# Exponentials straight out of PSUM for the last five tiles of a decoder block's expert stage

## The reference

```
q = (x @ Wq + bq) as 8 heads of 64;  q = batchnorm(q)
q0, q1 = l2norm(q[..., :32]), l2norm(q[..., 32:])
s0, s1 = q0 . k0, q1 . k1                      # 32 scores each, per token and head
ts0, ts1 = the 4 largest of s0, of s1
w  = softmax over the 16 sums ts0[i] + ts1[j]
out = sum over heads and (i, j) of w * gelu(down[i*32+j] . x) * up[i*32+j]
```

## Time and profile before

| what | us |
|---|---|
| three runs | 439.9, 440.02, 441.66; median 440.02 |
| the profiled execution, its own time | 441.61 |
| its span, first to last instruction | 439.6 |
| busy: TensorE, VectorE, ScalarE, GpSimd | 406.9, 307.1, 228.6, 206.7 |
| mean granted TensorE clock | 0.984 of full speed |

### The profile page before, as it was taken

One profiled execution on the slowest core, in us unless ns is written; L12 is line 12 of the kernel. 1 busy time (PEld: TensorE's weight loads), 2 busy tenths in 40 slices (PEclk: granted clock), 3 DMA queues, 4 the chain that ended last, 5 costly groups with the idle time before them and its releaser, 6 DMA issues. The chain is left out here.

```text
span 439.6 us, 7801 instructions
## 1 busy us (share of the span) xinstructions
PE 406.9 (93%) x2579; PEld 371.9 (85%) x2579; DVE 307.1 (70%) x1133; ACT 228.6 (52%) x459; POOL 206.7 (47%) x201
## 2 busy tenths in 40 slices
PE   3998999978999999999999999999898978999786
PEld 2877788857899999999999999987686968999685
DVE  5899877568475576557647555575736698899995
ACT  3774546325565555445656443344555769675300
POOL 2588988922624234323332210001100659799991
PEclk9999999999999999999999999999999897999989
DMA  7700122002512222222222000000000000001011
GB/s 242 251 1 26 51 73 78 2 0 75 146 51 78 53 75 77 70 57 77 73 76 75 4 0 2 1 1 4 21 1 1 0 2 3 25 25 37 26 34 50
DMA packets 19991, 21.36 MB, mean 49 GB/s; under 512 B 3180, under 2 KB 16624, under 8 KB 19952
## 3 DMA queue, kind: packets, MB, share of 16 engines
q1 hardware_dynamic: 18832, 19.96, 15.4%
q10 hardware_dynamic: 1120, 0.92, 0.7%
HBM read 18.78 MB, written 2.10 MB: 47 GB/s over the span
## 5 line engine op out<-in xcount | busy, mean ns | idle before, releaser
L960 PE MATMUL att_pA<-context_cNh,att_pTh 128*128 128x256 f32 (+1 forms) x208 | 62.6, 301 | 1.0 <-DVE att_pTl L858 1.0
L961 PE MATMUL att_pA<-context_cNl,att_pTh 128*128 128x256 f32 (+1 forms) x208 | 58.3, 280 | 0.0
L962 PE MATMUL att_pA<-context_cNh,att_pTl 128*128 128x256 f32 (+1 forms) x208 | 58.1, 279 | 0.0
L1148 POOL TENSOR_TENSOR ffn_prod<-ffn_first,ffn_near 128x1024 f32<-128x1024 f32 (+1 forms) x29 | 54.7, 1885 | 6.4 <-DVE ffn_clamped L1499 5.9
L858 DVE TENSOR_TENSOR att_pTl<-att_pR,att_pTh 128x512 fp32r<-128x512 f32 x64 | 37.4, 586 | 26.7 <-ACT att_pTh L775 26.5
L877 DVE TENSOR_REDUCE att_mx<-keep_pQ 128x1 f32<-128x402 f32 x64 | 35.6, 568 | 25.5 <-PE keep_pQ L77 25.3
L765 POOL TENSOR_TENSOR context_cTl<-keep_raw,context_cTh 128x512 fp32r<-128x512 f32 (+1 forms) x24 | 23.1, 980 | 47.8 <-ACT context_cTh L789 47.8
L765 POOL TENSOR_TENSOR context_cNl<-keep_raw,context_cNh 128x512 fp32r<-128x512 f32 (+1 forms) x21 | 25.1, 1211 | 41.9 <-ACT context_cNh L789 41.9
L1634 PE MATMUL ffn_pT<-keep_ident,ffn_prod 128*128 128x128 f32 x256 | 34.8, 295 | 7.6 <-POOL ffn_prod L1148 6.3
L1634 PEld LDWEIGHTS ffn_pT<-keep_ident,ffn_prod 128*128 128x128 f32 x256 | 32.0, 153 | 10.8 <-DVE ffn_hT L1521 4.7
L960 PEld LDWEIGHTS att_pA<-context_cNh,att_pTh 128*128 128x128 f32 (+1 forms) x208 | 39.1, 188 | 2.2 <-DVE att_pTl L858 1.5
(11 more groups left out here) (302 smaller groups left out, 1145.6 us busy)
## 6 DMA issues: line engine op xcount, KB each, us to landing
keep_raw<-in_ctxT SPq DMA_DIRECT2D x24, 256.0 KB, 2.7
keep_raw<-in_ctx SPq DMA_DIRECT2D x24, 256.0 KB, 2.7
out<-keep_x SPq DMA_DIRECT2D x16, 128.0 KB, 1.7
keep_x<-in_x SPq DMA_DIRECT2D x3, 512.0 KB, 10.5
gru_wout<-in_W_out SPq DMA_DIRECT2D x1, 512.0 KB, 8.9
keep_raw<-in_fWq SPq DMA_DIRECT2D x2, 256.0 KB
keep_raw<-in_ctxT SPq DMA_DIRECT2D x8, 32.5 KB, 4.0
keep_raw<-in_ctx SPq DMA_DIRECT2D x4, 65.0 KB
```

The lines of the kernel that those rows point to most:

```text
L960: pe.matmul(pA[:, 0:D], l[0], r[0], start=(kt == 0), stop=False)
L961: pe.matmul(pA[:, 0:D], l[0], r[1], start=False, stop=False)
L962: last = pe.matmul(pA[:, 0:D], l[1], r[0], start=False, stop=(kt == CT - 1))
L1148: return eng.tensor_tensor(prod[:, i % PB, a:b].rearrange("p h (i j) -> p h i j", j=KEYS), (factor if factor is not None else first[:, n % ...
```

## The change

From tile 11 on (`RAISED_APART`), ScalarE takes the scores out of PSUM itself. It runs 16 exponentials of 128x32, one per head and half, each with that half's column of `ninv` as its scale, second halves first; then the Copy as before. VectorE's `scaled` is left out for these five tiles, and TensorE, before it overwrites a bank, waits for `raised` instead of `s_ready`. The wait for `near_ready` stands ahead of the branch, so it now comes before that for `s_ready` in the other tiles too.

```diff
--- before.py
+++ after.py
@@ -1120,6 +1120,7 @@
         SHARE = {LASTS - 1: HEADS // 2, LASTS: HEADS - 5, LASTS + 1: HEADS - 5}
         LATE_GELU = 6
         ADDED = TILES - WEIGH
+        RAISED_APART = 11
 
         def wait_squares(eng, n, chunks):
 
@@ -1290,9 +1291,23 @@
 
                 def exponentials(i):
                     n, t = i // PER, i % PER
-                    act.wait_ge(s_ready, i + 1)
                     if n >= 2:
                         act.wait_ge(near_ready, i - 2 * PER + 1)
+                    if i >= RAISED_APART:
+                        act.wait_ge(score_mm, i + 1)
+                        act.wait_ge(ninv_ready, [n in b for b in BATCHES].index(True) + 1)
+                        for part, done in ((1, e_ready), (0, raised)):
+                            for h in range(HEADS):
+                                g = 2 * h + part
+                                last = act.activation(e[:, n % 2, t, h, part * KEYS:(part + 1) * KEYS],
+                                                      pS[:, i % 2, g * KEYS:(g + 1) * KEYS], ACT.Exp,
+                                                      scale=ninv[:, i, g:g + 1])
+                            last.then_inc(done, 1)
+                        act.wait_ge(raised, i + 1)
+                        act.activation(e[:, n % 2, t, :, 0:KEYS], e[:, n % 2, t, :, 0:KEYS], ACT.Copy, scale=LIFT)\
+                            .then_inc(e_ready, 1)
+                        return
+                    act.wait_ge(s_ready, i + 1)
                     act.activation(e[:, n % 2, t, :, 0:KEYS], s[:, i % 2, :, 0:KEYS], ACT.Exp).then_inc(raised, 1)
                     act.activation(e[:, n % 2, t, :, KEYS:PAIR], s[:, i % 2, :, KEYS:PAIR], ACT.Exp).then_inc(e_ready, 1)
                     act.wait_ge(raised, i + 1)
@@ -1535,7 +1550,7 @@
                                                 *(inverse_norm_steps(k) for k in norm_batch if i > 2))
                     if i == TILES - 1:
                         steps = itertools.islice(final := weight_steps(n, 0, 1), 2)
-                    if 3 <= i + 1 < TILES:
+                    if 3 <= i + 1 < RAISED_APART:
                         scaled(i + 1)
                     dve.wait_ge(e_ready, 2 * i + 1)
                     largest(i, 1, steps)
@@ -1612,7 +1627,9 @@
 
                 def scores(i):
                     wait_query(pe, i // PER, QC)
-                    if i >= 2:
+                    if i - 2 >= RAISED_APART:
+                        pe.wait_ge(raised, i - 1)
+                    elif i >= 2:
                         pe.wait_ge(s_ready, i - 1)
                     for c in range(QC):
                         q = q0[:, c, i * P:(i + 1) * P] if i < PER else query(c, i * P, (i + 1) * P)
```

## The result

| | before | changed |
|---|---|---|
| median of the runs | 440.84 us (439.9 to 443.28, 4 runs) | 446.89 us (446.18 to 450.63, 4 runs) |
| ratio to before, 95% interval | 1 | 1.0114 [1.0061, 1.0167] |
| the same, a second series (e1 below) | 440.03 us (17 runs) | 447.64 us (6 runs), 1.0146 [1.0088, 1.0204] |
| profiled execution: time, span, granted clock | 441.61, 439.6, 0.984 | 450.63, 448.8, 0.973 |

The change makes the kernel slower, by the two ratios 5.0 and 6.4 us (the medians lie 6.1 and 7.6 apart). The forecast was 442.7 us with a range of 441.0 to 445.0: the sign was right, the size was not, and the time lies outside the range.

What follows compares the result with a forecast made beforehand. GpSimd was taken to set the pace after 379.79, 4.9 us a tile, fed by a chain through ScalarE and TensorE. Terms 0 + 1.3 + 1.36 = +2.7 us gave 442.7 us, range 441.0 to 445.0.

Steps and rivals of the forecast that it cites:

- the last bullet of Part 2: Tile 8: late exponential and squares make TensorE 0.9 us late, hidden by a longer stall at tile 11; 0.
- Part 2: Wait order in all tiles from 4 on: table load now stands behind the scaled scores; +1.3 us, all from tile 4.
- Part 3: Tile 11: sixteen exponentials ahead of the square root delay VectorE's reciprocal, so GpSimd's near is late; +1.36 us.
- Rival B: Second low clock stretch at TensorE's tile 8 norm sums; 2.6 for 1.36, or with late rise +4.8, 444.8 us; chance 0.16.
- Tile 4, forecast 1.3: Exponential of tile 4 starts 1.30 us later, delaying TensorE's sum of tile 1 and GpSimd; middle of 0.49 and 2.19.
- the forecast's upper case: Tile 4: clock stays low through the sum of tile 1 and eight score matmuls; TensorE late by 2.19 us.
- Its sign of being wrong: Last square root, tile 11: VectorE's reciprocal starting without a wait would show the sixteen-exponential step wrong.
- Part 1: VectorE's five scalings leave, 3.0 us of its time, absorbed by its waits for GpSimd's near; 0.
- Tile 6 and the rest of the order: Tile 6: its table load follows the GELUs, when the scores are already scaled; 0.
- A: Tile 4: clock rises at the same moment as before, 0.49+1.36 = +1.9, 441.9 us; chance 0.20.
- C: Table load does not wait behind the moved wait, exponentials every 0.12 us; 0 and 0.4, 440.4 us; chance 0.05.
- D: VectorE and not GpSimd is the bound, so its 3.0 us come back; faster, 437.0 us; chance 0.03.

Runs made afterwards that it cites:

- e1: The changed kernel run again without further edits, beside three variants on the same chip; 1.0146 of the kernel before.
- a1: Kernel before with only the wait order changed, near_ready called ahead of s_ready in every tile from 4 on; 1.0143 of the kernel before.
- a4: Kernel before with the two waits exchanged in tile 8 alone; 1.0090 of the kernel before.
- e2: Changed kernel with the old order of the two waits put back at tile 8 alone; 1.0082 of the kernel before.
- e4: Changed kernel with normalising and squares of group 6 moved ahead of the exponentials of tile 8; 1.0105 of the kernel before.
- d1: Changed kernel with eight matmuls nobody reads in TensorE's pause before the norm sums of group 6; 1.0096 of the kernel before.
- e3: Changed kernel with the old order of the two waits put back at tile 4 alone; 1.0121 of the kernel before.
- a3: Kernel before with the two waits exchanged in tile 4 alone; 1.0057 of the kernel before.
- a2: Changed kernel with the old wait order below tile 11, leaving only the sixteen exponentials and missing scalings of tiles 11 to 15; 1.0040 of the kernel before.
- b1: a4 with eight matmuls nobody reads put into TensorE's pause before the norm sums of group 6; 1.0016 of the kernel before.
- b2: As a2, but the exponentials are taken out of PSUM from tile 12 on instead of 11; 0.9991 of the kernel before.
- d2: a4 with normalising and squares of group 6 moved ahead of the exponentials of tile 8; 1.0016 of the kernel before.
- c1: Kernel before with the edits of b3 and b2 together; 0.9957 of the kernel before.
- b3: Kernel before with the last two GELUs moved ahead of the exponentials of tile 4, one table load fewer; 0.9950 of the kernel before.
- c2: b3 with TensorE's pauses before the sum of tile 0 and the norm sums of group 4 filled with unread matmuls; 0.9949 of the kernel before.
- c3: Kernel before with TensorE's pauses before the sums of tiles 0 and 1 filled with unread matmuls; 1.0000 of the kernel before.

## Why the prediction was wrong

- **The step that failed** is the last bullet of Part 2: "Part 3 stalls the same engines for longer at the next place, so it is hidden: 0". Up to there it is right in each number (the load behind the wait, the squares late, a pause of TensorE near 1 us: 1.13). What it left out is that the clock falls behind this pause, during the norm sums or within 0.5 us of their end. GpSimd is then 2.8 to 4.4 us late, more than Part 3's 1.36, and the cover works the other way round: Part 3 hides behind tile 8. The kernels with and without Part 3 show it: +4.40 (changed) and +4.48 (a1), +2.77 (e1) and +2.81 (a4). e2 and e4 show Part 3 alone, and d1 shows the forecast's own case: with the clock up, the delay of tile 8 is 1.22 us and hides behind Part 3, +1.37 in all. So the cover was right, and what tile 8 costs was wrong. This was Rival B, with 0.16. Its price for one low stretch, 2.6 in place of 1.36, is what e1 shows (+2.77), and its sum, 2.19+2.6 = 4.8, is near e1's 2.59+2.77 = 5.4. What it lacked is the stretch of twice that length (changed, a1, e3: +4.4), and the chance it deserved: the argument for it stood in the text. The place it took as its model isn't quite the same, though: ahead of 368.89 the norm sums came first (365.80 to 367.65, at the full clock) and the pause of 1.24 us behind them, and the clock fell in that pause, at about 368.6. At tile 8 the pause comes first.
- **Tile 4, forecast 1.3.** Mechanism right, and the size is one of two that occur, in part by luck: 1.3 was the middle between two cases (the clock rises at the same moment, 0.49; it stays down through the scores, 2.19), and in the changed kernel's trace neither holds. Counted from group 0's product, the sum of tile 1 starts 1.34 us later (forecast 1.30) and the clock rises 1.0 later than before. Seven profiles have the new order there: +1.2 to +1.4 in five (changed, a1, a3, d1, e4), +2.45 and +2.59 in e2 and e1, where the clock stays down through the sum of tile 1 and the scores, as in the forecast's upper case (2.19). Profiles without the new order there scatter too, from 22.4 to 23.1 us (before, a2, a4, b1, b2, d2, e3). I had this bound and kept it for the range, where it was a case of its own. a3's ratio gives 2.5 us, 0.9 to 4.1 by its interval.
- **Part 3, forecast 1.36,** was right where it can be seen: 1.30 to 1.38 us in a2, e4 and e2. The exponentials come every (2.96-0.29)/15 = 0.178 us, with the forecast's 0.29 for the length of one; forecast 0.18. Its sign of being wrong, a reciprocal without a wait, came true in the changed kernel all the same: there it means that Part 3 is covered, not that it is missing. The Trainium skill ("ScalarE: Activation LUTs", section "What ACT_TABLE_LOAD costs", and the same page's figures per column and operand) gave 1.38 us of drain beside each load and, as an estimate from those figures, 0.21 us for the pitch. The trace differs on both: 0.178, and the load at 365.10 is followed by the exponential at 366.40, 1.30 later. By its ratio a2 costs 1.8 us, from 0 to 3.5, which the distance does not contradict.
- **Part 1, nothing:** right (b2, 0.9991 [0.9961, 1.0020]).
- **Tile 6 and the rest of the order, nothing:** right within what a1 can tell, since a3 and a4 (2.5+4.0 = 6.5) add up to about a1's 6.3.
- **Rivals A, C, D.** A wanted +0.49 at tile 4, and no trace shows it. C fell with the first table load (365.10, behind the scores), D with b2 and c1.
- **The sum.** The two profiles of the change give 1.18+4.40 = 5.6 us and 2.59+2.77 = 5.4, and the ratios 5.0 and 6.4. Of the forecast 2.7, tile 8 was 1.4 to 3.0 short beyond Part 3, and tile 4 up to 1.3.

The best kernel of the study is b3, faster than both: 439.75 us beside 441.57, 0.9950 [0.9921, 0.9980].

## What to carry to other kernels

When a change delays an engine's input by a microsecond, look at what TensorE does next: here a pause of 1.13 us ahead of small matmuls cost 4.0 us (a4), where the same delay without the fall of the clock cost GpSimd 1.22 (d1). Moving the producer of their operand ahead gave it back (d2). Filling the pause gave most of it back on average (b1), but not in every execution. A loss may be called hidden behind another only when both are priced with their worst case: the larger is the visible one. And the order in which an engine's waits are called is a part of the change: the one called second stood here ahead of the table load and put 1.28 us behind the wait.

## What the runs showed of the hardware

- After the pause of 1.13 us the clock fell in five of five traces with this pause at group 6 (changed, a1, a4, e1, e3), during the sixteen norm sums of four columns or, in e1, 0.5 us behind them, for 3.4 us in two and 6.8 in three. In the eleven traces without a pause there (before, a2, a3, b2, b3, c1, c2, c3, d2, e2, e4) it did not fall. With the pause filled it stayed up in one (d1, 0.21 us left) and fell in the other (b1, 0.19 us left). Why it falls in one and not in the other is open.
- The stretches of low clock differ from run to run. Near 342, ahead of all that any of these kernels changes, the clock was low for 6.8 us in seven traces, for 3.4 in eight and not at all in three. The changed kernel's two profiled executions have distances of +1.18 and +4.40, and +2.59 and +2.77, and nearly the same sum. The kernel before, with one and the same code, ran from 439.5 to 445.8 us; how much of this spread is the clock isn't shown.
- ScalarE takes exponentials of 128x32 pieces out of PSUM with a factor per row at one every 0.178 us (sixteen in 2.96).
